# Moving one unit of row maxima between two key blocks of PV on TensorE

## The chip, the cores and the metric

The kernel runs on one core of a Trainium2 chip. The metric is device microseconds of that core, from the median of several runs. The engines are TensorE (PE in the profile; its weight loads are listed apart as PEld), VectorE (DVE), ScalarE (ACT), GpSimd (POOL) and SyncE (SP, which issues most of the DMAs). They run side by side and meet at semaphores. Lines such as L1384 are lines of the kernel before.

## The reference

A transformer layer on 2 sequences of 512 tokens with 128 features: a modulated projection, causal attention with 16 heads of 8 features, an output projection with residual, a mixture of shared and routed experts, and a mixture of zones. The change touches attention alone:

```python
scores = jnp.einsum('bhsd,bhtd->bhst', q, k) / scale
causal = jnp.tril(jnp.ones((S, S), dtype=bool))
scores = jnp.where(causal[None, None], scores, -jnp.inf)
attn = jax.nn.softmax(scores.astype(jnp.float32), axis=-1).astype(x.dtype)
out = jnp.einsum('bhst,bhtd->bhsd', attn, v)
...
x = x + _L0_attn_ref(_L0_cond_ref(x, cond_1024, L0_cond_weight), L0_attn_w_qkv, L0_attn_w_out)
```

## The kernel before

The 2 sequences and 16 heads make 8 groups of four heads (`GROUPS`, `HG`), and the 512 tokens are four blocks of 128 (`KB`). Attention runs in 8 periods, n = 0 to 7. In period n three groups are under way at once:

- Scores for the exponential of group n, with keys along the partitions (`scores_for_exp`, L1422, L1426, L1431). There are six pieces, u = 0 to 5. Each goes through one of two pairs of PSUM banks, so piece u waits until ScalarE's exponential (`exp`, L1089) of piece u - 2 is done. This text calls them E0 to E5.
- Row maxima of groups n+1 and n+2, with queries along the partitions (`scores_for_max`, L1384, L1389). TensorE makes a unit of scores in one of three ring banks (`RING_BANKS`), and VectorE adds the mask and reduces it (`reduce_max`, L753). A unit waits until VectorE has reduced the unit three places earlier in the ring. From group 2 on a group has eleven units, and the last of them, number 10, is the one with the diagonal blocks of token block 0 of all four heads: one matmul of 512 columns (L1384), four reductions of 128 columns. This text calls it the diagonal unit. After it VectorE places the group's maxima (`place_max`, L766, L768), and TensorE lays them under the queries (`lay_max_under_q`, L1399), which ScalarE copies out (`copy_qm`, L1093).
- PV of group n-1 (`weigh_v`, L1447): probabilities times values, key block by key block, all into one bank. The four heads take 32 columns of the array each and run at the same time. A float32 matmul is done in two passes, so a key block shows as 8 matmuls in the trace, in two halves of four. Block 0 is done in period n-1, blocks 1, 2 and 3 in period n. When block 3 is done, ScalarE copies the bank out (`copy_pv`, L1099), between E1's exponential and E2's.

`maximum(i)`, i = 0 to 10, issues a period's share of units (`max_units`). In periods 1 to 6 `maximum(3)` is exactly the diagonal unit of group n+1. In period 0 it is an ordinary unit and there is no PV of an earlier group; in period 7 it is empty. The order on each engine is the order in which the code is written; nothing reorders it. The part of a period that matters here, on TensorE:

```python
scores_for_exp(n, 1)
maximum(1)
maximum(2)
if n:
    weigh_v(n - 1, 1, P, S)
    weigh_v(n - 1, 2, 2 * P, S)
    weigh_v(n - 1, 3, 3 * P, S)
maximum(3)
scores_for_exp(n, 2)
...
scores_for_exp(n, 3)
maximum(4)
maximum(5)
maximum(6)
scores_for_exp(n, 4)
```

`maximum(4)` to `maximum(6)` are units 0, 1 and 2 of group n+2; unit 2 is three places behind the diagonal unit in the ring. After E4 come PV block 0 of group n, unit 3, the laying of the maxima, unit 4, E5, unit 5 (three places behind unit 3, the laying counts as a place) and unit 6.

Of the kernel before, what the change touches and what calls it, by code (L numbers as in the profile page):

```python
# [68 lines left out]
def max_units(n, i):  # L69

    first, end = units_to(n + 1, LEAD if n else FIRST), units_to(n + 2, LEAD)
    return MX_LIST[first + (end - first) * i // SLICES:first + (end - first) * (i + 1) // SLICES]
# [78 lines left out]
def program(nc, io, scratch, out):  # L151
# [9 lines left out]
    with ctx:  # L161
# [1101 lines left out]
        def _(pe):  # L1263
# [103 lines left out]
            def scores_for_max(n, u):  # L1367
                s = n % 2
                pieces = MX_UNITS[n][u]
                if n == 0:  # L1370
                    if u < 2 * HG:
                        pe.wait_ge(q0_placed, u + 1)
                    if u in (0, HG):
                        pe.wait_ge(rep_copied, 1 + u // HG)
                elif u == 0:
                    pe.wait_ge(q_padded[s], 16 * HG * ((n + 1) // 2))
                    pe.wait_ge(ld_stack[n][1], 16)
                wait_ring("max", n, u)
                bank = ring("max", n, u)
                if len(pieces) == HG:  # L1380
                    pe.wait_ge(ld_stack[n][0], 16)
                    for padded in k_padded[n % BUFS]:
                        pe.wait_ge(padded, 32 * (n // BUFS + 1))
                    last = T.matmul(bank.rearrange("p (j k) -> p j k", j=HG), q_mov[n % BUFS][0:TOP, 0:P],  # L1384
                                    k_pad[n % BUFS][0:TOP, :, 0:P], start=True, stop=True)
                else:
                    for j, qb, o in pieces:
                        width = max(2 * P, P * (qb + 1))
                        last = T.matmul(bank[:, o:o + width], q_pad[s][0:TOP, j, qb * P:(qb + 1) * P],  # L1389
                                        stacked[0:TOP, n, 0:width], start=True, stop=True)  # L1390
                last.then_inc(mx_full, 1)

            def lay_max_under_q(n):
                pe.wait_ge(m_ready, n + 1)
                wait_ring("lay", n)
                if n == 0:
                    pe.wait_ge(const_ready, 1)
                for qb in range(KB):
                    last = T.matmul(ring("lay", n)[:, qb * P:(qb + 1) * P], max_pad[n % 2][:, qb, :], ident_b[:],  # L1399
                                    start=True, stop=True)  # L1400
                last.then_inc(qm_full, 1)

            def scores_for_exp(n, u):
                s = n % BUFS
                c, h2 = divmod(u, 2)
                if u == 0:
                    pe.wait_ge(qm_copied, n + 1)
                    if n == 0:
                        pe.wait_ge(rep_copied, 4)
                    else:  # L1410
                        pe.wait_ge(ld_stack[n][0], 16)
                    if n < BUFS:
                        pe.wait_ge(ones_rows[s], 16)
                if c == 0:
                    pe.wait_ge(k_padded[s][h2], 32 * (n // BUFS + 1))
                wait_slot("exp", n, u)
                at_ = slot_of("exp", n, u)
                q = q_mov[s][0:ROWS, :]
                if c < 2:
                    for i in range(2):  # L1420
                        k = k_pad[s][0:ROWS, 2 * h2 + i, c * P:(c + 1) * P]
                        last = T.matmul(ST[:, at_ + i, 0:S - c * P], k, q[:, c * P:S], start=True, stop=True)  # L1422
                elif h2 == 0:
                    for j in range(HG):
                        o = j % 2 * 2 * P
                        last = T.matmul(ST[:, at_ + j // 2, o:o + 2 * P], k_pad[s][0:ROWS, j, 2 * P:3 * P], q[:, 2 * P:S],  # L1426
                                        start=True, stop=True)
                else:
                    pe.wait_ge(q1_zero, 2)
                    pe.wait_ge(q_last_ready, n + 1)  # L1430
                    last = T.matmul(ST[:, at_, :].rearrange("p (j q) -> p j q", j=HG), stacked[0:ROWS, n, 3 * P:S],  # L1431
                                    q_last[0:ROWS], start=True, stop=True)
                last.then_inc(st_full, 1)

            def weigh_v(n, kb, lo, hi):
                c = min(kb, 2)
                pe.wait_ge(masked, 3 * n + c + 1)
                if kb == 0 and lo == 0:
                    pe.wait_ge(v_copied, KB * (n // NG + 1))
                    if n:  # L1440
                        pe.wait_ge(pv_copied, n)
                    else:
                        pe.wait_ge(xc_ready[2], 1)
                o = lo - kb * P + (2 * P if kb == 3 else 0)
                for j in range(HG):
                    v0 = ((n * KB + kb) * HG + j) * VC
                    last = T.matmul(PV[32 * j:32 * j + 32, lo:hi], v_all[:, v0:v0 + 32],  # L1447
                                    probs[n % 2][:, c, j, o:o + hi - lo], start=(kb == 0 and lo == 0),
                                    stop=(kb == KB - 1), skip_group_check=True)
                if kb == KB - 1:  # L1450
                    last.then_inc(pv_full, 1)
# [25 lines left out]
            def project_out(b):  # L1477
                pe.wait_ge(onorm_ready, b + 1)
                pe.wait_ge(ld_small, 16)
                if b == 0:  # L1480
                    wait_ring("out", 0)
                    T.matmul(ring("out", 0), small[:, W_OUT:W_OUT + D], packed_out[:],
                             start=True, stop=True).then_inc(proj_ready, 1)
                else:
                    pe.wait_ge(last_norm, 1)
                    T.matmul(MISC, small[0:EARLY, W_OUT:W_OUT + D], packed_out[0:EARLY, :], start=True, stop=False)
                    T.matmul(MISC, small[:, W_LAST:W_LAST + D], o_sb[1][:], start=False,
                             stop=True).then_inc(proj_ready, 1)
# [15 lines left out]
            def route_experts(b):  # L1504
                pe.wait_ge(temb_ready, B)
                pe.wait_ge(x1_ready, b + 1)
                if b == 0:
                    wait_ring("route", 0)
                bank = ring("route", 0) if b == 0 else MISC
                T.matmul(bank[:, 0:KB * EXPERTS], temb[:, b, :], small[:, W_RT:W_RB], start=True, stop=True)  # L1510
                for t in range(KB):
                    last = T.matmul(bank[:, t * EXPERTS:(t + 1) * EXPERTS],
                                    x1[:, b * S + t * P:b * S + (t + 1) * P], small[:, W_R:W_RT],
                                    start=False, stop=True, skip_group_check=True)
                last.then_inc(logits, 1)
# [99 lines left out]
            for n in range(GROUPS):  # L1615

                def maximum(i):
                    for unit in max_units(n, i):
                        scores_for_max(*unit)

                scores_for_exp(n, 0)
                maximum(0)
# [3 lines that stand above are left out]
                if n:  # L1626
                    weigh_v(n - 1, 1, P, S)
                    weigh_v(n - 1, 2, 2 * P, S)
                    weigh_v(n - 1, 3, 3 * P, S)
                maximum(3)  # L1630
                scores_for_exp(n, 2)
                if n == GROUPS - 1:
                    project_out(0)
# [5 lines that stand above are left out]
                if n == GROUPS - 1:  # L1639
                    route_experts(0)  # L1640
                weigh_v(n, 0, 0, S)
                maximum(7)
                if n + 1 < GROUPS:
                    lay_max_under_q(n + 1)
                if n == 0:
                    project_v(1)
                maximum(8)
                scores_for_exp(n, 5)
                maximum(9)
                maximum(10)  # L1650
# [109 lines left out]
```

## Time and profile before

| what | value |
|---|---|
| median of 3 runs | 188.44 us |
| lowest and highest | 186.72 and 188.64 us |
| the profiled execution | 187.13 us |
| its span, first to last instruction | 185.4 us |
| TensorE busy | 171.9 us (93%) |
| VectorE busy | 148.0 us (80%) |
| ScalarE busy | 134.4 us (72%) |
| GpSimd busy | 93.9 us (51%) |

The span is what the trace covers; the 1.7 us between it and the execution's own time lie around it. Attention takes the span's part from about 25 to 97 us, the experts and zones what follows. A timeline row gives the start, the length, the engine, the line, the shapes and a count where equal instructions are merged; in brackets the idle time of the engine just before and what ended it.

### The profile page before, as it was taken

What the parts mean: (1) busy time and instruction counts of PE and PEld (TensorE: products, weight loads), DVE (VectorE), ACT (ScalarE), POOL (GpSimd) and SP (SyncE); (2) the same over time, 40 slices, a digit from 0 to 9 for tenths busy, and PEclk for the clock granted to TensorE, in tenths of its full rate; (3) what the DMA queues carried; (4) which work ended last, traced back from release to release, by engine and by line L of the source; (5) the groups of instructions that cost most, each with busy time, mean ns of one, the idle gap of its engine ahead of it and who ended that gap; (6) DMA issues with size and microseconds to landing.
All of it is one profiled execution on the core that took longest, in us unless ns stands there. A gap on an engine that the chain in (4) does not pass through costs nothing.

```text
span 185.4 us, 3258 instructions
## 1 busy us (share of the span) xinstructions
PE 171.9 (93%) x934; PEld 118.1 (64%) x934; DVE 148.0 (80%) x458; ACT 134.4 (72%) x224; POOL 93.9 (51%) x102
## 2 busy tenths in 40 slices
PE   7998989899999999989999999896996999999993
PEld 2755565565666667653658767674674867788881
DVE  5589899879898899992697998798999847656652
ACT  4569267667777888889634986945559999799980
POOL 4509086894453858587422522022838980677000
PEclk9999999999999999999999999999699999999998
DMA  4824765757666657520122999930940000001001
GB/s 140 284 44 107 200 175 142 226 182 243 190 216 187 170 185 192 170 81 1 57 53 66 257 333 319 347 91 11 280 167 0 0 4 0 0 2 57 0 4 57
DMA packets 15205, 24.28 MB, mean 131 GB/s; under 512 B 2700, under 2 KB 4684, under 8 KB 15164
## 3 DMA queue, kind: packets, MB, share of 16 engines
q1 hardware_dynamic: 14388, 23.29, 41.4%
q10 hardware_dynamic: 800, 0.79, 1.6%
q8 instruction: 8, 0.13, 0.3%
q14 instruction: 9, 0.07, 0.1%
HBM read 18.71 MB, written 5.27 MB: 129 GB/s over the span
## 4 chain that ended last, share of the span: by engine, by line
PE 59%; issue 10%; DVE 8%; POOL 8%; ACT 6%; SPq 5%; DMA 2%; POOLq 0%; DVEq 0%; ACTq 0%
PE psum L1519 9%; PE psum L1389 8%; PE psum L1520 8%; PE psum L1521 8%; PE psum L1447 8%; PE psum L1422 6%; POOL t_q_pad L686 3%; ACT t_probs L1089 2%; SPq L430 2%; SPq L443 2%; PE psum L1325 2%; PE psum L1271 2%; DMA scratch<-t_dn_lo 2%; PE psum L1384 1%; PE psum L1426 1%
## 5 line engine op out<-in xcount | busy, mean ns | idle before, releaser
L753 DVE CUSTOM_DVE_ANT_0 psum<-psum,t_causal 128x128 f32<-128x128 f32 (+3 forms) x128 | 58.7, 521 | 4.7 <-PE psum L1384 2.6
L1089 ACT ACTIVATE t_probs<-psum 128x1024 f32<-128x1024 f32 (+2 forms) x48 | 40.7, 882 | 8.9 <-PE psum L1422 5.2
L1389 PE MATMUL psum<-t_stacked,t_q_pad 96*128 96x256 f32 (+2 forms) x104 | 31.9, 377 | 2.2 <-DVE t_row_max L753 1.0
L655 POOL TENSOR_SCALAR_AFFINE_SELECT t_probs<-t_probs 128x512 f32<-128x512 f32 x32 | 20.9, 666 | 22.7 <-ACT t_probs L1089 20.7
L1389 PEld LDWEIGHTS psum<-t_stacked,t_q_pad 96*128 96x128 f32 x104 | 17.7, 188 | 16.3 <-DVE t_row_max L753 11.1
L928 DVE SCALAR_TENSOR_TENSOR t_q_pad<-psum,t_zw_all,t_q_pad 128x512 fp32r<-128x512 f32 x24 | 17.9, 749 | 10.2 <-ACT t_q_pad L1137 10.2
L1447 PE MATMUL psum<-t_probs,t_v_all 128*32 128x512 f32 (+3 forms) x256 | 20.8, 439 | 0.4 <-POOL t_probs L655 0.4
L686 POOL TENSOR_TENSOR t_q_pad<-t_raw,t_q_pad 128x512 fp32r<-128x512 f32 x8 | 10.7, 1344 | 20.3 <-ACT t_q_pad L1139 20.3
L753 DVE DVE_READ_ACCUMULATOR2_ANT t_row_max<- 128x1 f32 x128 | 18.0, 140 | 0.0
L1137 ACT ACTIVATE t_q_pad<-psum,t_zw_all 128x512 fp32r<-128x512 f32 x24 | 16.6, 690 | 0.8
L1123 ACT ACTIVATE t_raw<-psum 128x512 f32<-128x512 f32 x24 | 14.3, 598 | 3.7 <-PE psum L1521 3.6
L915 DVE TENSOR_TENSOR psum<-t_raw,t_stacked 128x512 f32<-128x512 f32 x16 | 15.2, 956 | 0.7 <-DVE t_top L836 0.7
L1519 PE MATMUL psum<-t_stacked,t_up_hi 128*128 128x512 f32 x32 | 14.3, 446 | 0.8 <-DVE t_q_pad L931 0.7
L1123 ACT ACTIVATE psum<-psum 128x512 f32<-128x512 f32 x24 | 14.1, 588 | 0.0
L1422 PE MATMUL psum<-t_q_two,t_k_pad 104*128 104x512 f32 (+1 forms) x48 | 13.6, 382 | 0.4 <-ACT t_q_two L1093 0.4
L1520 PE MATMUL psum<-t_stacked,t_up_lo 128*128 128x512 f32 x32 | 12.8, 401 | 0.0
L1521 PE MATMUL psum<-t_stacked,t_up_hi 128*128 128x512 f32 x32 | 12.8, 401 | 0.0
L1447 PEld LDWEIGHTS psum<-t_probs,t_v_all 128*32 128x32 f32 x256 | 6.4, 109 | 8.6 <-POOL t_probs L655 3.4
L1139 ACT CAST t_q_pad<-psum 128x512 fp32r<-128x512 f32 x16 | 9.4, 587 | 3.1 <-DVE psum L915 2.7
L1519 PE MATMUL psum<-t_q_pad,t_dn_hi 128*128 128x512 f32 x24 | 10.0, 416 | 1.7 <-ACT t_probs L1149 1.6
L931 DVE TENSOR_TENSOR t_q_pad<-psum,t_q_pad 128x512 fp32r<-128x512 f32 x16 | 10.9, 678 | 0.8 <-ACT t_q_pad L1139 0.8
L1422 PEld LDWEIGHTS psum<-t_q_two,t_k_pad 104*128 104x128 f32 x48 | 8.5, 189 | 2.4 <-issue 0.9
(230 smaller groups left out, 378.1 us busy)
## 6 DMA issues: line engine op xcount, KB each, us to landing
t_stacked<-scratch SPq DMA_DIRECT2D x16, 256.0 KB, 5.4
t_probs<-in_L_ffn_Wa SPq DMA_DIRECT2D x2, 1024.0 KB, 12.5
scratch<-t_o_sb SPq DMA_DIRECT2D x7, 256.0 KB, 2.1
t_raw<-in_experts SPq DMA_DIRECT2D x7, 256.0 KB, 3.2
t_stacked<-scratch SPq DMA_DIRECT2D x9, 192.0 KB, 2.8
t_q_pad<-scratch SPq DMA_DIRECT2D x28, 48.0 KB
scratch<-t_dn_hi SPq DMA_DIRECT2D x2, 512.0 KB, 3.3
t_q_two<-scratch SPq DMA_DIRECT2D x5, 192.0 KB, 2.5
```

The costliest lines, as they stand in the source:

```text
L655: last = G.affine_select(out=tri, in_=tri, compare_op=ALU.is_ge, fill=0.0, base=0, pattern=[[0, HG], [1, P]], channel_multiplier=-1)
L753: last = V.tensor_tensor_reduce(scores, scores, causal[:, S - width:S], 1.0, 3 * BIG, ALU.add, ALU.max, row_max[s][:, qb, j:j + 1])
L928: V.scalar_tensor_tensor(h_lo[i % SLOTS], hidden_of(i), weight_of(i), f32_of(h_hi[i % SLOTS]), ALU.mult, ALU.subtract).then_inc(lo_done, 1)
L1089: A.activation(o, scores, ACT.Exp, scale=float(1.0 / np.sqrt(np.float32(HD)))).then_inc(exp_done, 1)
L1123: A.activation(o, pair_of(i)[:, 0, :], func, scale=scale).then_inc(act_done, 1)
L1137: A.activation(h_hi[i % SLOTS], hidden_of(i), ACT.Identity, scale=weight_of(i)).then_inc(hi_done, 1)
L1389: last = T.matmul(bank[:, o:o + width], q_pad[s][0:TOP, j, qb * P:(qb + 1) * P], stacked[0:TOP, n, 0:width], start=True, stop=True)
L1422: last = T.matmul(ST[:, at_ + i, 0:S - c * P], k, q[:, c * P:S], start=True, stop=True)
L1447: last = T.matmul(PV[32 * j:32 * j + 32, lo:hi], v_all[:, v0:v0 + 32], probs[n % 2][:, c, j, o:o + hi - lo], start=(kb == 0 and lo == 0), ...
L1519: T.matmul(o, hi, x_hi, start=start, stop=False)
L1520: T.matmul(o, lo, x_hi, start=False, stop=False)
L1521: return T.matmul(o, hi, x_lo, start=False, stop=stop)
```

## The change

The diagonal unit is written between PV blocks 2 and 3 in place of behind block 3:

```diff
                 if n:
                     weigh_v(n - 1, 1, P, S)
                     weigh_v(n - 1, 2, 2 * P, S)
+                maximum(3)
+                if n:
                     weigh_v(n - 1, 3, 3 * P, S)
-                maximum(3)
                 scores_for_exp(n, 2)
```

TensorE in period 4, at the place of the edit (L1447 is PV, block 2 with 256 columns and block 3 with 128; L1384 is the diagonal unit; L1422 is E2; in brackets the semaphores waited for):

```order
 L1447 MATMUL psum<-t_probs,t_v_all 32x256 [waits masked]
 L1447 MATMUL psum<-t_probs,t_v_all 32x256 x3
-L1447 MATMUL psum<-t_probs,t_v_all 32x128 [waits masked]
-L1447 MATMUL psum<-t_probs,t_v_all 32x128 x3
 L1384 MATMUL psum<-t_stacked 128x512 [waits k_padded2a,k_padded2b,ld_stackq5,mx_reduced]
+L1447 MATMUL psum<-t_probs,t_v_all 32x128 [waits masked]
+L1447 MATMUL psum<-t_probs,t_v_all 32x128 x3
 L1422 MATMUL psum<-t_q_two,t_k_pad 128x384 [waits exp_done]
 L1422 MATMUL psum<-t_q_two,t_k_pad 128x384
```

The unit now stands with matmuls of 32 columns on both sides, and block 3 with matmuls of 128 columns on both sides. The same difference stands in periods 1, 2, 3, 5 and 6, six in all, and nowhere else.

What follows on TensorE in period 4, the same before and after the change (L1389 are units 0, 1 and 2 of the next group, L1426 is E4, L1447 is PV block 0):

```order
 L1389 MATMUL psum<-t_stacked,t_q_pad 128x256 [waits mx_reduced]
 L1389 MATMUL psum<-t_stacked,t_q_pad 128x256
 L1389 MATMUL psum<-t_stacked,t_q_pad 128x384 [waits mx_reduced]
 L1426 MATMUL psum<-t_q_two,t_k_pad 128x256 [waits exp_done]
 L1426 MATMUL psum<-t_q_two,t_k_pad 128x256 x3
 L1447 MATMUL psum<-t_probs,t_v_all 32x512 [waits pv_copied,v_copied,masked]
```

Nothing moved here. The 384-column unit waits for VectorE to reduce the diagonal unit, and L1426 waits for ScalarE's exponential of E2.

ScalarE in period 4, the same before and after the change (L1099 is the copy of PV, L1089 are exponentials, L1184 is a copy for the experts):

```order
L1089 ACTIVATE t_probs<-psum 128x1024 [waits st_full]
L1099 COPY t_o_sb<-psum 128x512 [waits stored1,pv_full]
L1089 ACTIVATE t_probs<-psum 128x2x384 [waits st_full]
L1184 CAST t_up_hi<-t_raw 128x512 [waits ld_raw2]
L1089 ACTIVATE t_probs<-psum 128x2x384 [waits st_full]
```

Nothing moved here either: the copy that waits for PV block 3 stands ahead of E2's exponential.

## Rows read from the trace of the kernel before

**Rows 1.** Busy time of each engine in period 4 (windows).
```profile
core 0: us, PE busy (x) PEld busy (x) DVE busy (x) ACT busy (x) POOL busy (x), PEclk, DMA share, GB/s
61.07:69.44 8.37, 8.36 (x64) 5.34 (x63) 7.76 (x35) 7.06 (x11) 5.95 (x7) 1.00 0.56 163
```

**Rows 2.** The chain that ended last, from 60 to 72 us, by line.
```profile
by line: PE psum L1389 38.0%; PE psum L1447 26.6%; PE psum L1422 21.5%; PE psum L1399 4.0%; PE psum L1426 3.9%; PE psum L1431 3.9%; PE psum L1384 3.6%; issue 0.1%
```

**Rows 3.** Timeline of PE in period 4, E1 to unit 5.
```profile
61.92 0.64 PE L1422 MATMUL psum<-t_q_two,t_k_pad 104*128 104x512 f32 x2
62.40 0.63 PE L1389 MATMUL psum<-t_stacked,t_q_pad 96*128 96x512 f32 x2
62.96 1.50 PE L1447 MATMUL psum<-t_probs,t_v_all 128*32 128x384 f32 x24
64.39 0.50 PE L1384 MATMUL psum<-t_stacked 96*128 96x512 f32 x1
64.73 0.87 PE L1422 MATMUL psum<-t_q_two,t_k_pad 104*128 104x384 f32 x4
65.44 1.08 PE L1389 MATMUL psum<-t_stacked,t_q_pad 96*128 96x256 f32 x5
66.36 0.63 PE L1426 MATMUL psum<-t_q_two,t_k_pad 104*128 104x256 f32 x4
66.92 1.06 PE L1447 MATMUL psum<-t_probs,t_v_all 128*32 128x512 f32 x8
67.92 0.44 PE L1389 MATMUL psum<-t_stacked,t_q_pad 96*128 96x384 f32 x1
...
69.08 0.68 PE L1389 MATMUL psum<-t_stacked,t_q_pad 96*128 96x384 f32 x2
```

**Rows 4.** Timeline of the weight loads (PEld), period 4.
```profile
63.30 0.13 PEld L1447 LDWEIGHTS psum<-t_probs,t_v_all 128*32 128x32 f32 x4 [0.19 <-issue]
63.63 0.56 PEld L1447 LDWEIGHTS psum<-t_probs,t_v_all 128*32 128x32 f32 x12 [0.19 <-issue]
64.06 0.13 PEld L1447 LDWEIGHTS psum<-t_probs,t_v_all 128*32 128x32 f32 x4
64.39 0.19 PEld L1384 LDWEIGHTS psum<-t_stacked 96*128 96x128 f32 x1 [0.20 <-issue]
...
66.08 0.19 PEld L1389 LDWEIGHTS psum<-t_stacked,t_q_pad 96*128 96x128 f32 x1 [0.22 <-DVE t_row_max L753]
```

**Rows 5.** Timeline of DVE, period 4: the diagonal unit, then unit 3.
```profile
64.93 0.30 DVE L753 CUSTOM_DVE_ANT_0 psum<-psum,t_causal 128x128 f32<-128x128 f32 x1 [0.53 <-PE psum L1384]
...
65.89 0.14 DVE L753 DVE_READ_ACCUMULATOR2_ANT t_row_max<- 128x1 f32 x1
...
68.39 0.58 DVE L753 CUSTOM_DVE_ANT_0 psum<-psum,t_causal 128x384 f32<-128x384 f32 x1
68.89 0.14 DVE L753 DVE_READ_ACCUMULATOR2_ANT t_row_max<- 128x1 f32 x1
```

**Rows 6.** Timeline of ACT, period 4: copy of PV, exponential of E2.
```profile
64.53 0.59 ACT L1099 COPY t_o_sb<-psum 128x512 f32<-128x512 f32 x1 [0.67 <-PE psum L1447]
65.28 0.81 ACT L1089 ACTIVATE t_probs<-psum 128x768 f32<-128x768 f32 x1 [0.17 <-PE psum L1422]
```

**Rows 7.** Timelines of PE and ACT, period 6: E2, E4, E2's exponential.
```profile
81.48 0.86 PE L1422 MATMUL psum<-t_q_two,t_k_pad 104*128 104x384 f32 x4
82.90 0.74 PE L1426 MATMUL psum<-t_q_two,t_k_pad 104*128 104x256 f32 x4 [0.56 <-ACT t_probs L1089]
...
82.03 0.81 ACT L1089 ACTIVATE t_probs<-psum 128x768 f32<-128x768 f32 x1 [0.17 <-PE psum L1422]
```

**Rows 8.** Timelines of PE and DVE, period 1: unit 3 and its reduction.
```profile
42.59 0.44 PE L1389 MATMUL psum<-t_stacked,t_q_pad 96*128 96x384 f32 x1
...
43.24 0.60 DVE L753 CUSTOM_DVE_ANT_0 psum<-psum,t_causal 128x384 f32<-128x384 f32 x1
```

**Rows 9.** Timeline of SP's queue, period 4: the query loads for group 7.
```profile
69.16 1.61 SPq L430 DMA_DIRECT2D t_q_pad<-scratch  x4
```

## The prediction

> **What bounds the kernel now.** I read the windows first, one period of attention at a time. In period 4 TensorE is busy for 8.36 of 8.37 us and VectorE for 7.76 [rows 1], and the chain that ended last runs from 60 to 72 us over TensorE's lines alone [rows 2]. So the time of a period is the time of TensorE's list, and what counts is what its starts hide: the ends of matmul rows are modelled, the starts are not. I therefore read differences of starts. Two 512-column matmuls take 0.48 us (61.92 to 62.40), 0.24 each; four of 384 take 0.71 (64.73 to 65.44), 0.18 each [rows 3]. Against these, four places cost more than their columns.
>
> Switch in, from 128 to 32 columns: the last two units before PV take 62.40 to 62.96, 0.56 where 0.48 is their price, so 0.08. By the same 0.08 the four 256-column matmuls of E4 (66.36 to 66.92) are 0.12 each [rows 3]. The first tiled half of PV then takes 0.34 (62.96 to 63.30) and the second 0.33 (to 63.63), 0.01 more [rows 3, 4].
>
> Switch out, from 32 to 128: the loads for the second half of block 3 start at 64.06, when its first half starts to stream. Two halves of block 2 took 0.43 (63.63 to 64.06), so two of block 3, with half the columns, take 0.22 and end at 64.28. The diagonal unit's weights load only from 64.39: 0.11 later [rows 4].
>
> Uncovered load: a matmul whose weights were not loaded under the one before costs 0.10 more. The diagonal unit takes 0.34 (64.39 to 64.73) where 0.24 is the price [rows 3].
>
> The wait for VectorE: TensorE is through unit 1 at 65.44 + 4 x 0.12 = 65.92, but unit 2 needs the diagonal unit reduced, and that ends at 65.89 + 0.14 = 66.03. Its load starts at 66.08 and it streams at 66.18, 0.26 after it could have [rows 3 to 5]. VectorE for its part sat idle 0.53 us until the diagonal unit was there [rows 5].
>
> **The change, part by part.** Nothing is added or removed; per period one matmul of 512 columns changes places with eight of 128. VectorE's, ScalarE's, GpSimd's and SP's lists stay as they are.
>
> The diagonal unit comes earlier. Block 2 ends at 64.06, the switch out takes 0.11, so its load starts at 64.17 in place of 64.39. Its reductions move by the same 0.22, within VectorE's idle 0.53, and end at 65.81.
>
> TensorE's list gets longer, by one more pass in each direction. From 64.17: unit 0.34, switch in 0.08, block 3 0.01 + 0.22, switch out 0.11, uncovered load of E2 0.10. E2 streams at 65.03 in place of 64.73: **0.30 us later**. Before, E2's weights were loaded under the diagonal unit; that cover is gone.
>
> The Trainium skill's page "TensorEngine Tiling (Array Packing)", section "Tiling Modes", says that changing the tiling mode, not just the tile, drains TensorE. It speaks against this change, gives no price, and the 0.08 and 0.11 above are what a switch shows in this trace. The page "TensorE: Matmul & The Clock Gate", section "Single matmul latency", puts a drain at about 175 ns; as an estimate from that figure the two added switches would cost 0.35 in place of 0.19, and the change 1 us more over six periods. No row shows so much, and the rows decide.
>
> The wait at unit 2 goes. TensorE is there at 65.92 + 0.30 = 66.22, VectorE done at 65.81, and unit 2's weights load under unit 1. It streams at 66.22 in place of 66.18. Up to here the period loses 0.04 in place of 0.30.
>
> What is late next is E4. It uses the banks of E2 and waits for ScalarE's exponential of it. Before, that ended at 65.28 + 0.81 = 66.09, just in time to load E4 under unit 2 [rows 6]. Now it starts 0.30 later by E2, at 65.58. Ahead of it on ScalarE stands the copy of PV, which waits for block 3, and block 3 ends at 64.82 in place of 64.28, 0.54 later. So the copy starts at 64.53 + 0.54 = 65.07, occupies ScalarE for 0.58 (64.53 to 65.28, less the 0.17 idle before 65.28), and lets the exponential start at 65.65. It ends between 66.39 and 66.46. In period 6, where E4 waits for it already, the load follows 0.06 after the exponential's end (82.03 + 0.81 to 82.90) [rows 7]. So E4 loads at 66.45 to 66.52, uncovered, and streams 0.10 later, at 66.55 to 66.62 in place of 66.36: **0.19 to 0.26 us a period**.
>
> Behind E4 nothing gives it back. PV block 0 and unit 3 follow; unit 3's scores are ready at 67.92 + 0.44 = 68.36, VectorE starts on them at 68.39 and ends at 68.89 + 0.14 = 69.03, and unit 5 starts at 69.08 [rows 3, 5]. This piece hangs on unit 3 alone, so it moves as a whole. Earlier reductions before it only turn into a longer wait at unit 5.
>
> Of DMAs only the store of the PV copy moves, by 0.54. Queued behind it on SP are among others the query loads for group 7, issued by 69.16 + 1.61 = 70.77 [rows 9]. They are used by unit 0 of period 5, one period after 65.44, at 73.8 [rows 1, 3], which itself gets later. I count them as nothing; without that 3 us of cover each 0.1 us would cost 0.1.
>
> The sum. Periods 2 to 5 are alike: 4 x 0.19 to 0.26 is 0.76 to 1.04. In period 6 E4 waits for the exponential anyway (idle 0.56) [rows 7], so nothing is absorbed: 0.30, or 0.37 if the copy comes last. In period 1 VectorE started on unit 3 at 43.24 although it was ready at 42.59 + 0.44 = 43.03; less the 0.03 of reaction it had 0.18 in hand and now comes earlier, so that period pays 0.01 to 0.08 [rows 8]. Periods 0 and 7 are untouched. Together 1.07 to 1.49; I take the middle, 1.3, since copy and E2 come within 0.07 of each other. Everything after attention depends on what precedes it and moves along. The profiled execution would take 187.13 + 1.3 = 188.4, the median 188.44 + 1.3 = **189.7 us**.
>
> **The rivals.** Slower by more: block 3 alone is short. Its halves of 0.11 are shorter than the loading of four weights, 0.13 in the rows of 63.30 and 64.06 [rows 4]. In the middle of PV these loads are hidden under longer halves; behind the diagonal unit up to 0.12 more could stand open, at most one load of 0.13 less the 0.01 counted. That delays block 3, the copy and E2 alike, 0.12 x 6 = 0.7: 190.4 in all. It decides from about 0.1 a period, where the loss passes 1%. Against it: the first half of block 1 showed only 0.01.
>
> Not slower, first: the switch is hidden. If the diagonal unit's weights could load under block 2 and block 3's under the unit, E2 would not move, the wait at unit 2 would go, and E4 would start when the exponential lets it: loading 0.06 after 66.09, streaming at 66.25, 0.11 earlier. Five periods give -0.55: 187.9. The row of 64.39 speaks against it, since that load waited although nothing but the switch held it ("issue", 0.20) [rows 4]. The page on TensorE, section "Step-by-step: what each phase is for", says that weight loads are pulled ahead of matmuls in flight when they go to the background buffer; by that rule this rival would hold, and the trace agrees only among matmuls of one kind.
>
> Not slower, second: VectorE is the real pace. Then its 0.22 comes off each of periods 1 to 5, and period 6 pays 0.30: -0.8, 187.6. For it speaks the wait at unit 2, against it the idle 0.53 on VectorE and that unit 5 hangs on unit 3.
>
> That the change doesn't do what it says is excluded by the order: the swap stands in six periods.
>
> **How the numbers follow.** Forecast 0.67, the short block 3 0.20, hidden switch 0.07, VectorE's pace 0.06. The runs before lie between 186.72 and 188.64, so a median may be off by some 0.7 and this kernel hardly tells less than 1% (1.9 us) from no change. The range takes the forecast and the first rival: from 189.5 less the scatter and some room, 188.3, to 190.4 plus some scatter, 190.8. Slower by over 1% means above 190.3: half of the first rival and some scatter of the forecast, 0.21. Faster by over 1% needs more than either rival gives, 0.03. Within 1%: 0.76.
>
> **What the profile after would show.** In periods 2 to 5 the diagonal unit's row starts some 0.33 after block 2's last half started; a second gap of about 0.1 opens in front of E2; unit 2 has no idle time behind VectorE; E4 (L1426) has some, ended by ScalarE's L1089; a period takes about 8.6 us. I am wrong if E2's load is covered, if E4 shows no wait, or if the period grows by the full 0.30.

## The result, and the profile after

The changed kernel took 190.82 us in the median of 5 runs (190.56 to 192.14), the kernel before 188.61 in 5 (186.72 to 190.83): a ratio of 1.0187 with a 95% interval of 1.0125 to 1.0249. It is slower, by more than was forecast, and its median lies 0.02 us above the range. Its profiled execution took 192.14 us, with a span of 190.4 us. Here and below a ratio goes by the times near the fastest of each kernel, medians and means go by all times, so a ratio is not their quotient (1.0117 for these two medians).

Yet attention did what was forecast. Busy time of each engine in periods 2 to 4 of the changed kernel, each from the start of E5 to the next (windows):

```profile
core 0: us, PE busy (x) PEld busy (x) DVE busy (x) ACT busy (x) POOL busy (x), PEclk, DMA share, GB/s
45.91:54.51 8.60, 8.58 (x64) 5.13 (x63) 7.92 (x35) 6.17 (x9) 3.51 (x5) 1.00 0.52 164
54.51:63.07 8.56, 8.55 (x63) 5.12 (x63) 7.91 (x35) 6.57 (x10) 4.03 (x6) 1.00 0.59 172
63.07:71.64 8.57, 8.55 (x63) 5.13 (x63) 7.92 (x35) 7.01 (x11) 5.95 (x8) 1.00 0.63 189
```

A period is 0.20 us longer (8.57 against 8.37 [rows 1]), and TensorE is busy all through it. Periods 3 to 5 take 8.56 to 8.60 us in every trace of the changed kernel. The timeline of TensorE in period 4, changed kernel:

```profile
65.18 0.62 PE L1389 MATMUL psum<-t_stacked,t_q_pad 96*128 96x512 f32 x2
65.73 1.28 PE L1447 MATMUL psum<-t_probs,t_v_all 128*32 128x384 f32 x16
66.94 0.50 PE L1384 MATMUL psum<-t_stacked 96*128 96x512 f32 x1
67.38 0.43 PE L1447 MATMUL psum<-t_probs,t_v_all 128*32 128x128 f32 x8
67.73 0.96 PE L1422 MATMUL psum<-t_q_two,t_k_pad 104*128 104x384 f32 x4
68.53 0.80 PE L1389 MATMUL psum<-t_stacked,t_q_pad 96*128 96x256 f32 x5
69.25 0.72 PE L1426 MATMUL psum<-t_q_two,t_k_pad 104*128 104x256 f32 x4
```

Its weight loads, and VectorE's and ScalarE's timelines at the same place:

```profile
66.40 0.13 PEld L1447 LDWEIGHTS psum<-t_probs,t_v_all 128*32 128x32 f32 x4 [0.19 <-issue]
66.94 0.19 PEld L1384 LDWEIGHTS psum<-t_stacked 96*128 96x128 f32 x1 [0.41 <-DVE t_row_max L753]
67.37 0.16 PEld L1447 LDWEIGHTS psum<-t_probs,t_v_all 128*32 128x32 f32 x8 [0.25 <-issue]
67.73 0.65 PEld L1422 LDWEIGHTS psum<-t_q_two,t_k_pad 104*128 104x128 f32 x4 [0.20 <-issue]
...
69.25 0.30 PEld L1426 LDWEIGHTS psum<-t_q_two,t_k_pad 104*128 104x128 f32 x2 [0.17 <-ACT t_probs L1089]
...
65.75 0.14 DVE L753 DVE_READ_ACCUMULATOR2_ANT t_row_max<- 128x1 f32 x1
...
67.48 0.30 DVE L753 CUSTOM_DVE_ANT_0 psum<-psum,t_causal 128x128 f32<-128x128 f32 x1 [0.30 <-PE psum L1384]
71.38 0.57 DVE L753 CUSTOM_DVE_ANT_0 psum<-psum,t_causal 128x384 f32<-128x384 f32 x1 [0.26 <-PE psum L1389]
...
67.87 0.59 ACT L1099 COPY t_o_sb<-psum 128x512 f32<-128x512 f32 x1 [1.26 <-PE psum L1447]
68.39 0.81 ACT L1089 ACTIVATE t_probs<-psum 128x768 f32<-128x768 f32 x1
```

The reader is to see four things. The unit (66.94) and block 3 (67.37, 67.38) each start behind a gap of their own, and E2's weights load only at 67.73, when its matmul is due. The bracket of 66.94 names VectorE, but the reduction that the unit has to wait for, three places earlier in the ring, was over at 65.75 + 0.14 = 65.89, so VectorE does not make this gap. Unit 2 no longer stands behind VectorE: the five L1389 from 68.53 run on, where one waited until 66.08 before [rows 3, 4]. E4's weights wait 0.17 for ScalarE's L1089, which they did not before. And VectorE still waits, now also 0.26 us at 71.38 for unit 3, so its earlier start is worth nothing behind E4.

Where the rest of the time went is seen in windows at places that the change doesn't touch. Changed kernel:

```profile
18.70:25.50 6.80, 6.68 (x16) 3.60 (x14) 3.70 (x13) 1.18 (x5) 2.05 (x2) 0.50 0.78 193
145.00:148.40 3.40, 3.40 (x9) 2.65 (x10) 3.23 (x7) 2.30 (x5) 3.32 (x3) 0.51 0.00 0
```

Kernel before, the first of these stretches:

```profile
18.70:25.50 6.80, 5.87 (x28) 3.53 (x27) 6.10 (x29) 2.37 (x6) 2.40 (x2) 1.00 0.84 215
```

The column PEclk is the granted clock. At 0.50, the lower of the two levels, TensorE got through 16 matmuls where it did 28 at full clock. The first stretch lies ahead of the first moved instruction, and it alone puts E4 of period 0 at 32.29 us in place of 29.88.

### The profile page after: what moved, and what is told of

Read it like the earlier page. It is cut to its first block, busy times and chain, and to the rows that moved or that the text cites. A ratio compares the mean times of both kernels' runs of the same rounds, so it can differ in the third digit from the quotient of the medians.

```text
span 190.4 us, 3258 instructions
## 1 busy us (share of the span) xinstructions
PE 175.4 (92%) x934; PEld 118.4 (62%) x934; DVE 148.7 (78%) x458; ACT 133.9 (70%) x224; POOL 93.8 (49%) x102
## 4 chain that ended last, share of the span: by engine, by line
PE 64%; DVE 14%; issue 7%; ACT 7%; POOL 6%; POOLq 0%; DVEq 0%; ACTq 0%
PE psum L1389 9%; PE psum L1519 9%; PE psum L1447 8%; PE psum L1520 8%; PE psum L1521 8%; PE psum L1422 7%; DVE psum L753 5%; POOL t_q_pad L686 4%; PE psum L1339 3%; ACT t_probs L1089 2%; PE psum L1325 2%; PE psum L1271 2%; PE psum L1426 2%; PE psum L1384 1%; PE psum L1349 1%
## 5 line engine op out<-in xcount | busy, mean ns | idle before, releaser
L1089 ACT ACTIVATE t_probs<-psum 128x1024 f32<-128x1024 f32 (+2 forms) x48 | 40.8, 882 | 7.7 <-PE psum L1422 5.1
L1389 PE MATMUL psum<-t_stacked,t_q_pad 96*128 96x256 f32 (+2 forms) x104 | 32.1, 390 | 2.0 <-DVE t_row_max L753 1.2
L1389 PEld LDWEIGHTS psum<-t_stacked,t_q_pad 96*128 96x128 f32 x104 | 18.3, 199 | 16.2 <-DVE t_row_max L753 10.2
L1447 PE MATMUL psum<-t_probs,t_v_all 128*32 128x512 f32 (+3 forms) x256 | 21.8, 441 | 0.0
L915 DVE TENSOR_TENSOR psum<-t_raw,t_stacked 128x512 f32<-128x512 f32 x16 | 14.6, 917 | 1.8 <-ACT t_raw L1123 1.0
L1422 PE MATMUL psum<-t_q_two,t_k_pad 104*128 104x512 f32 (+1 forms) x48 | 14.0, 390 | 0.4 <-ACT t_q_two L1093 0.4
L1447 PEld LDWEIGHTS psum<-t_probs,t_v_all 128*32 128x32 f32 x256 | 5.9, 108 | 8.2 <-issue 4.3
L1422 PEld LDWEIGHTS psum<-t_q_two,t_k_pad 104*128 104x128 f32 x48 | 8.2, 188 | 3.0 <-issue 1.7
```

Source lines behind the costliest of these rows:

```text
L1089: A.activation(o, scores, ACT.Exp, scale=float(1.0 / np.sqrt(np.float32(HD)))).then_inc(exp_done, 1)
```

## The experiments

Each ran against the kernel before on the same chip. The table gives the mean and the ratio with its interval, and from the one trace of each the time from E5 of period 1 to E5 of period 7 (attention, which leaves out period 1), from there to the end (behind), and the start of E4 of period 0 (head). In e_best the new order stands in period 0 too, so its head is not comparable.

| run | times | mean us | ratio (95%) | head | attention | behind |
|---|---|---|---|---|---|---|
| before, first profile | | | | 29.88 | 49.22 | 92.44 |
| changed, first profile | 5 | 191.09 | 1.0187 (1.0125 to 1.0249) | 32.29 | 50.51 | 93.97 |
| c_before | 12 | 189.28 | 1.0073 (1.0017 to 1.0128) | 32.17 | 49.25 | 93.99 |
| c_before_2 | 12 | 188.23 | 1.0003 (0.9956 to 1.0051) | 32.15 | 49.24 | 92.46 |
| c_after | 6 | 190.24 | 1.0140 (1.0047 to 1.0234) | 29.92 | 50.32 | 94.03 |
| c_after_2 | 6 | 189.80 | 1.0100 (1.0038 to 1.0163) | 29.96 | 50.38 | 94.00 |
| c_after_3 | 12 | 189.69 | 1.0109 (1.0066 to 1.0151) | 32.17 | 50.55 | 93.97 |
| e_mid | 12 | 189.77 | 1.0110 (1.0056 to 1.0164) | 32.27 | 50.60 | 93.99 |
| e_switch | 6 | 189.47 | 1.0130 (1.0045 to 1.0215) | 29.88 | 50.84 | 92.47 |
| e_five | 12 | 190.02 | 1.0073 (1.0027 to 1.0120) | 29.96 | 50.09 | 93.99 |
| e_best | 12 | 189.47 | 1.0060 (1.0020 to 1.0099) | 29.16 | 49.77 | 94.04 |
| e_delay | 6 | 190.12 | 1.0103 (1.0018 to 1.0188) | 31.91 | 50.55 | 93.97 |
| e_delay_2 | 6 | 189.64 | 1.0110 (1.0034 to 1.0187) | 29.80 | 50.51 | 92.44 |
| e_early | 12 | 188.02 | 1.0030 (0.9989 to 1.0071) | 30.69 | 48.96 | 93.99 |
| f_before | 12 | 188.31 | 1.0009 (0.9950 to 1.0069) | 29.89 | 49.25 | 93.03 |
| f_after | 12 | 188.43 | 1.0016 (0.9972 to 1.0059) | 31.97 | 50.54 | 92.49 |
| f_early | 12 | 187.09 | 0.9948 (0.9904 to 0.9991) | 30.08 | 49.19 | 92.46 |

**The control and the changed kernel again.** No edit.

> The kernel before, unchanged, as a control for scatter. Theory A (the change costs what its attention periods show, 6 periods at about 0.19, some 1.1 us; the rest of the 2.2 us between the first medians is where stretches of the lower TensorE clock happen to fall): single times spread over some 4 us, as 186.7 to 190.8 did, and the periods 2 to 5 take 8.37 to 8.39 us. Theory B (the change costs another 1 us or more outside attention in every execution): the times of this kernel stay near 188.6.

> The changed kernel, unchanged, once more. Theory A: periods 2 to 5 take 8.57 us again, outside attention its stretches of full clock are as long as before's, and its median lies 1.0 to 1.3 us above the control's, a ratio of about 1.006. Theory B: the median lies 2.2 to 3.5 us above the control's again, a ratio of 1.012 to 1.019, and a stretch outside attention is longer at full clock.

> The kernel before once more, to compare with the changed kernel on the same chip. Theory A (the change costs its attention periods, 1.2 us; where the stretches of the lower TensorE clock fall is chance, the same for both kernels): single times between 186 and 191 us in groups about 1.5 us apart, and behind attention either 92.4 or 94.0 us, by whether a stretch of the lower clock falls on busy matmuls at about 143 to 148 us. Theory B (the change itself costs more behind attention): always 92.4.

> The changed kernel once more. Theory A: from the end of period 1 to the end of period 7 it takes 1.1 to 1.3 us more than the kernel before, and everything else is one of the same few values (ahead of attention 29.9 or 32.2 us, behind it 92.4 or 94.0); over all times of both kernels the difference comes towards 1.2 us, 0.6 to 0.7%. Theory B: behind attention 94.0 us always, and 2 us or more between the kernels.

> The changed kernel once more. If the 0.6 us between its mean excess so far (1.8) and what attention shows in each trace (1.1 to 1.3) is chance, these times are on average 1.2 us above the kernel before, with some below 188; if it belongs to the change, 1.8 us or more, with none below 188.

The kernel before, compared with itself, came out at 1.0073 with an interval that leaves out 1, and the second time at 1.0003; its single times in all jobs lie between 186.09 and 191.14 us. Its trace in c_before has both lower stretches that the changed kernel's first trace had (windows, kernel before, execution of c_before):

```profile
18.00:25.00 7.00, 6.88 (x17) 3.79 (x16) 4.19 (x14) 1.10 (x6) 1.82 (x5) 0.52 0.79 178
...
144.00:148.00 4.00, 4.00 (x12) 3.13 (x11) 3.58 (x7) 2.93 (x6) 3.92 (x4) 0.57 0.00 0
```

So those two are no property of the change. Its other trace, of c_before_2, has the lower clock behind attention elsewhere, and full clock where c_before had the lower one:

```profile
130.90:134.90 4.00, 4.00 (x13) 2.78 (x12) 3.97 (x4) 2.37 (x5) 3.27 (x3) 0.58 0.86 275
144.00:148.00 4.00, 4.00 (x19) 3.23 (x18) 4.00 (x7) 3.76 (x7) 3.98 (x3) 1.00 0.00 0
```

The 14 traces without the fillers that come last below all have just one such stretch between attention and the last microseconds. In four it lies between 129 and 136 us and the part behind attention takes 92.44 to 92.47 us; in ten it lies between 142 and 149 us and that part takes 93.97 to 94.04.

The execution of c_before and the changed kernel's first have the same head (32.17 and 32.29) and the same part behind attention (93.99 and 93.97), and their spans are 189.1 and 190.4 us: 1.3 apart. Attention takes 49.22 to 49.25 us in three traces of the kernel before and 50.32 to 50.55 in four of the changed one, 1.07 to 1.33 more. Theory A has its numbers there. That all four traces of the changed kernel have 94.0 behind attention is what theory B had.

Now the times. Over 133 of the kernel before (mean 188.55) and 29 of the changed one (190.07) the difference is 1.52 us, give or take 0.49 at 95%. Without the first five of each, which raised the question, it is 1.31, give or take 0.52, over 24 times of the changed kernel: near attention's value, and 2 lies outside. Each execution also has a mean granted clock. Among those with at most 0.973 the changed kernel lies 1.06 above the kernel before (8 and 40 times, give or take 0.53), among the others 1.36 (16 and 88 times, give or take 0.39). The expectations for single jobs were met in part. In the first job c_after came out at 1.0140, as theory B had it, though the control beside it was at 1.0073, and their medians (190.18 and 189.11) are 1.07 apart, as theory A had it. The mean of c_after_3 is 1.3 above that job's 23 times of the kernel before (188.36), but none of the 12 lies below 188.

In the two traces of the changed kernel at full clock up to attention, E5 to E5 of period 2 takes only 8.42 and 8.44 us (windows of periods 2 and 3, c_after):

```profile
43.89:52.31 8.42, 8.42 (x63) 5.13 (x63) 7.78 (x35) 6.00 (x9) 3.51 (x5) 1.00 0.58 174
52.31:60.87 8.56, 8.55 (x63) 5.12 (x63) 7.93 (x35) 6.58 (x10) 4.03 (x6) 1.00 0.59 169
```

That is the marker: in period 2 E5 comes 0.17 earlier before unit 5, which waits longer for VectorE behind it.

**The unit between blocks 1 and 2.**

```diff
                 if n:
                     weigh_v(n - 1, 1, P, S)
+                maximum(3)
+                if n:
                     weigh_v(n - 1, 2, 2 * P, S)
                     weigh_v(n - 1, 3, 3 * P, S)
-                maximum(3)
```

> The diagonal unit between PV blocks 1 and 2 in place of 2 and 3. As many switches as in the changed kernel, but both parts of PV are long. If the price is the switches and the uncovered load of E2 (0.30), with E4 then waiting for E2's exponential, a period takes 8.57 us as in the changed kernel, since an earlier diagonal unit helps nothing that ends last. If the short block 3 on its own was part of the price, a period takes up to 0.1 less, about 8.47.

Periods 2 to 5 took 8.60, 8.63, 8.58 and 8.60 us. With both parts of PV long the price is the same, so no part of it is seen to come from the short block 3.

**Another unit between blocks 1 and 2.**

```diff
-                maximum(2)
                 if n:
                     weigh_v(n - 1, 1, P, S)
+                maximum(2)
+                if n:
                     weigh_v(n - 1, 2, 2 * P, S)
```

> The kernel before with another unit, the last of maximum(2) (512 columns), moved from ahead of PV to between blocks 1 and 2; the diagonal unit stays behind block 3. This adds the same pass out of and into 32 columns without the earlier diagonal unit. By the price per switch (0.11 out, 0.10 uncovered load, 0.08 + 0.01 in) TensorE's list grows by 0.30, and the wait for VectorE at unit 2 moves along, so nothing is absorbed: a period of 8.68 us, 6 x 0.30 = 1.8 us in all. If the switches cost little and the changed kernel's 0.19 came from E2's exponential alone, a period stays at 8.38 to 8.45.

Windows of periods 3 and 4 of this kernel, E5 to E5:

```profile
52.47:61.19 8.72, 8.70 (x64) 5.24 (x63) 7.88 (x35) 6.66 (x10) 4.35 (x6) 1.00 0.58 175
61.19:69.90 8.71, 8.69 (x64) 5.22 (x63) 7.88 (x35) 7.04 (x11) 5.93 (x8) 1.00 0.60 172
```

8.71 us, 0.34 more than before where 0.30 was worked out. The pass out of 32 columns and back costs that by itself; the changed kernel, at 8.57, gets 0.14 of it back through the wait at unit 2. From E4 of period 0 to E5 of period 7 it takes 64.73 us, 1.67 more than the kernel before, where 1.8 was expected.

**The swap in periods 1 to 5 alone.**

```diff
                     weigh_v(n - 1, 2, 2 * P, S)
+                if n < GROUPS - 2:
+                    maximum(3)
+                if n:
                     weigh_v(n - 1, 3, 3 * P, S)
-                maximum(3)
+                if n >= GROUPS - 2:
+                    maximum(3)
```

> The swap in periods 1 to 5 alone; period 6 keeps the diagonal unit behind block 3. Periods 2 to 5 as in the changed kernel, 8.57 us. From E5 of period 5 to E5 of period 6 it took 7.55 us before and 8.06 with the change, 0.51 more. If that is period 6's own swap (0.30 to 0.37) and a wait carried over from period 5 (unit 5 behind E5, about 0.17), it takes 7.72 here; if it is all the swap's, 7.55.

From E5 of period 5 to E5 of period 6 it took 7.72 us, to the hundredth what was expected:

```profile
78.13:85.85 7.72, 7.16 (x57) 4.10 (x56) 7.52 (x27) 6.84 (x10) 5.45 (x7) 1.00 0.36 125
```

Of the 0.51 that the changed kernel loses there, 0.34 are period 6's swap and 0.17 come over from period 5.

**One PV group behind E2 and the diagonal unit.**

```diff
                 maximum(2)
+                scores_for_exp(n, 2)
+                maximum(3)
                 if n:
                     weigh_v(n - 1, 1, P, S)
                     weigh_v(n - 1, 2, 2 * P, S)
                     weigh_v(n - 1, 3, 3 * P, S)
-                maximum(3)
-                scores_for_exp(n, 2)
...
+                maximum(4)
                 scores_for_exp(n, 3)
-                maximum(4)
                 maximum(5)
-                maximum(6)
                 scores_for_exp(n, 4)
...
-                weigh_v(n, 0, 0, S)
+                maximum(6)
                 maximum(7)
+                weigh_v(n, 0, 0, S)
...
-                if 0 < n < GROUPS - 1:
-                    copy_pv(n - 1)
                 exp(n, 2)
+                if 0 < n < GROUPS - 1:
+                    copy_pv(n - 1)
```

> One group of PV as before, so no added switch, but the diagonal unit still earlier than in the kernel before: E2 stands ahead of the diagonal unit, both ahead of PV blocks 1 to 3; units 0 to 3 are spread around E3 and E4, PV block 0 comes behind unit 3, and ScalarE copies PV behind E2's exponential. If the switches (0.19) and the uncovered load (0.10) are what the changed kernel paid, and the wait at unit 2 and E4's wait for E2's exponential what the kernel before left open, a period takes about 8.22 us, and the time is some 0.6 to 1.0 us below the kernel before. If the earlier diagonal unit is worth nothing, a period stays at 8.38.

Periods 2 to 4 took 8.21, 8.20 and 8.22 us, as expected: without added switches the new order is worth 0.17 a period. It moves E2 as well as the diagonal unit, so what the earlier unit gives by itself is not shown. The whole was not quicker: 189.47 in the mean is 0.9 above the kernel before, with 94.0 behind attention. Period 5 took 8.69 and period 7 8.82 where they took 8.37 and 8.17 before. The timelines of SP's queue and of TensorE show why in the first case:

```profile
65.86 0.34 SPq L463 DMA_DIRECT2D scratch<-t_o_sb  x1
...
69.89 1.61 SPq L430 DMA_DIRECT2D t_q_pad<-scratch  x4
...
73.84 0.50 PE L1389 MATMUL psum<-t_stacked,t_q_pad 96*128 96x256 f32 x2 [0.42 <-DMA t_q_pad<-scratch]
```

Unit 0 waits for the query loads of group 7, the ones of [rows 9]. They stand behind the store of PV (L463), whose copy is later here. Their last issue ends at 71.50, and the unit starts 2.3 us later. In period 7 E2, now ahead of PV, waits 0.42 us for an exponential (87.48).

**The same in periods 1 to 4 only.** The edit is that of e_best under `if 1 <= n <= 4`, with the order of the kernel before elsewhere.

> As e_best in periods 1 to 4 (E2 and the diagonal unit ahead of one undivided PV, period of 8.21 us there), as the kernel before in the others, where e_best met a late load of queries in period 5 (0.42) and a worse order in period 7 (0.65). Periods 2 to 4 at 8.21 us give 0.5 us, periods 5 to 7 stay as before: from E5 of period 1 to E5 of period 7 about 48.7 us against 49.2, and a time about 0.5 us below the kernel before. If the earlier diagonal unit is taken back by the return to the old order, 49.2.

Periods 2 to 4 took 8.22, 8.18 and 8.22 us again, but period 5 took 8.57 and period 6 7.65 (8.37 and 7.55 before), so half of it was given back: attention 48.96 us in place of 48.7. In the mean 188.02, 0.53 below the 133 times of the kernel before, give or take 0.53.

**A later end of attention without the swap.**

```diff
                 wait_slot("exp", n, u)
                 at_ = slot_of("exp", n, u)
                 q = q_mov[s][0:ROWS, :]
+                if (n, u) == (3, 2):
+                    for _ in range(24):
+                        T.matmul(ST[:, at_, 0:P], ident_b[:], ident_b[:], start=True, stop=True)
```

> The kernel before with 24 matmuls of 128 bf16 columns in front of E2 in period 3 (they write a bank that E2 overwrites, and compute nothing that is used), so that attention ends about 1.2 us later and nothing else changes: no added switch. If a later end of attention costs its own length and no more, the mean over the runs lies 1.2 us above the kernel before. If moving the later work by 1.2 us makes it meet the lower TensorE clock more often, the mean lies about 1.8 us above, as the changed kernel's did (190.3 against 188.5 so far), with next to no time below 188.5, and the part behind attention takes 94.0 us.

> The same kernel as in e_delay again, for more times and a second trace; the same expectations.

Attention grew by 1.3 us, as much as the swap adds, and the part behind it took 93.97 us once and 92.44 once. The 12 times together have a mean of 189.88, 1.3 above the kernel before, with a standard error of 0.36, so that both 1.2 and 1.8 are possible. So a longer attention does not force the slower part behind it; whether it makes it more frequent is not told.

**TensorE kept at work in two waits behind attention.** In the kernel before, in the changed one and in e_early:

```diff
+            def fill(i, times):
+                pe.wait_ge(act_done, i - RING + 1)
+                for _ in range(times):
+                    T.matmul(pair_of(i)[:, 0, 0:P], ident_b[:], ident_b[:], start=True, stop=True)
+
             def zone_logits(b):
+                if b == 0:
+                    fill(AT["zone logits"][0], 18)
                 pe.wait_ge(z_tanh, b + 1)
...
             def zone_spread(b):
+                if b == 0:
+                    fill(AT["zone spread"][0], 24)
                 pe.wait_ge(z_w, b + 1)
```

> The kernel before with matmuls that keep TensorE at work in the two waits of the first zone choice (18 and 24 of 128 bf16 columns, ahead of the zone logits and of the spread of the zone weights, where it sat idle 1.40 and 1.77 us; they write a bank that the next unit overwrites, and nothing of them is used). If the 94.0 us that some executions take behind attention come of the lower clock that follows these waits, they vanish: 92.4 us always, no time of 190 us or more, and a mean of 187.7 us. If the lower clock does not depend on what TensorE did there, the two values stay.

> The changed kernel with the same matmuls in the same waits. If the change costs only its attention periods, it now lies 1.1 to 1.3 us above f_before in the mean (188.9), with the part behind attention at 92.4 us. If the change costs more for another reason, 1.6 us or more above f_before (189.3 or more).

> e_early with the same matmuls in the same waits. It should be the quickest of all: attention 0.3 to 0.5 us shorter than the kernel before, 92.4 us behind attention, a mean of 187.3 us. If the filling brings nothing, 188.0 as e_early.

Before, TensorE sat idle 1.77 us ahead of the spread of the weights (timeline, kernel before in c_before), and the lower clock of 144 to 148 us followed:

```profile
143.30 0.38 PE L1612 MATMUL psum<-t_zw,t_ones_row 1*128 1x3 f32 x2 [1.77 <-DVE t_zw L886]
```

The same wait, of 1.67 to 1.76 us, was followed by full clock in the four traces with the earlier stretch, so it does not decide by itself. In f_after there is little idle time left at that place:

```profile
141.61 1.51 PE L1609 MATMUL psum<-t_ident_b 128*128 128x128 bf16 x24
143.53 0.38 PE L1622 MATMUL psum<-t_zw,t_ones_row 1*128 1x3 f32 x2 [0.41 <-DVE t_zw L886]
```

The part behind attention took 93.03, 92.49 and 92.46 us in the three traces; 94.0 did not come up. f_before's trace has the earlier stretch, at 129 to 133 us, ahead of both fillers, so only the other two show a part behind attention without one, up to the last microseconds. No time of the 36 reaches 190 us, as 26 of the 133 of the kernel before do. The swap is in f_after, and behind attention it has the quick value: the swap alone does not make 94.0, and the ten traces above tie that value to the later stretch of the lower clock.

The means missed the expectations: f_before took 188.31 in place of 187.7, and f_after lies only 0.11 above it, give or take 0.78, where 1.1 to 1.3 was expected, which is outside, though attention still takes 50.54 against 49.25 us in the traces. Six of f_before's 12 times, and two of f_after's, have a mean granted clock of 0.982 or less; f_after's own trace, with the lower stretch in the head, has 0.982. So f_before probably met that stretch more often; whether this is all of the gap is not shown. f_early was the quickest of all and beat the kernel before in its own job at 0.9948 (0.9904 to 0.9991). Its trace doesn't credit the order of attention with that (49.19 against 49.22, the gain of three periods lost again in period 5, 8.73 us). The filled waits alone do not explain it either, since f_before has them too; only one of f_early's 12 times has a mean clock of 0.982 or less. What part is fillers and what part chance is open.

## Why the prediction was wrong, and where it held

The step that failed is the allowance for scatter, that a median may be off by some 0.7, and with it the last step of the sum, that everything after attention moves along. The 133 times of the kernel before have a standard deviation of 1.5 us, and medians of five drawn from them one of 0.9, so the difference of two such medians has 1.3. The part behind attention takes 92.4 or 94.0 us in single executions of the same kernel. The sum itself held:

- Switch out: block 2 ends 0.43 after 66.40 and the unit loads at 66.94, 0.11 as put. Switch in with the unit: 66.94 to 67.38, 0.44 for 0.42. Block 3 with its switch out: 67.38 to 67.73, 0.35 for 0.34. E2 uncovered: its four take 0.80 in place of 0.71, 0.09 for 0.10. From the first PV matmul to E2's streaming it is 2.10 (65.73 to 67.73, and 0.10 for the load) where it was 1.77: 0.33 for 0.30.
- The wait at unit 2 went, and E4 came next, as forecast: it loads at 69.25, 0.05 after the exponential's end (68.39 + 0.81), and streams 3.62 us after the first PV matmul in place of 3.40, 0.22 for 0.19 to 0.26.
- The copy of PV and E2 came within hundredths of each other; the exponential follows the copy without idle time.
- Period 1 was put at 0.01 to 0.08 and took about 0.15 at full clock: unit 5 starts at 44.14 in c_after and at 43.95 before, with heads of 29.92 and 29.88.
- The query loads were counted as nothing, with 3 us of cover. They landed in time, but by e_best's wait some 2.3 us of that is their landing, which leaves, as an estimate, 0.7.
- Period 6 lost 0.32 up to E4, with nothing absorbed. The timelines of TensorE there, kernel before and changed kernel, against [rows 7]:

```profile
79.71 1.50 PE L1447 MATMUL psum<-t_probs,t_v_all 128*32 128x384 f32 x24
...
82.90 1.28 PE L1447 MATMUL psum<-t_probs,t_v_all 128*32 128x384 f32 x16
...
86.41 0.74 PE L1426 MATMUL psum<-t_q_two,t_k_pad 104*128 104x256 f32 x4 [0.55 <-ACT t_probs L1089]
```

E4 stands 3.51 us behind the first PV matmul (82.90 to 86.41), where it stood 3.19 (79.71 to 82.90 [rows 7]). From E4 of period 0 to E5 of period 7 the whole is 64.29 and 64.32 us in c_after and c_after_2, 63.06 in the kernel before, all three at full clock: 1.23 to 1.26 where 1.07 to 1.49 was summed and 1.3 taken.

What came on top, 0.9 us between the first medians, was not attention. The forecast read one trace of the kernel before that happened to have its lower clock where it costs little (head 29.88, behind 92.44), and three times between 186.7 and 188.6. In truth the same kernel takes 186.1 to 191.1 us. Of the first five times of the changed kernel four have a mean granted clock of 0.970 to 0.973, as 8 of its later 24 have and 40 of 128 of the kernel before. In the later 24 the executions of the two kinds lie 1.9 us apart (191.15 and 189.21 in the mean), so this alone comes, as an estimate, to about 0.9. All five are at 190.56 or more, which only 7 of the later 24 are, so that independent chance would seldom bring them together; why they came in one job stays open. That the swap shifts the later work so that it meets the lower clock more often was neither shown nor excluded. All four of the changed kernel's own traces have 94.0 behind attention, and one of three of the kernel before.

Of the rivals, the short block 3 fell with e_mid, the hidden switch with e_switch. VectorE's pace fell: in the changed kernel the unit came earlier and the period grew. That the waits left something to gain was right: e_best's order, without the switches, shortens a period by 0.17.

The Trainium skill's page "TensorEngine Tiling (Array Packing)", section "Tiling Modes", has a change of tiling mode drain TensorE: e_switch agrees, where nothing else was added. The gaps here are 0.08 to 0.11 us, and 0.10 more is the weight load that is no longer covered. The estimate from the 175 ns of the Trainium skill's page "TensorE: Matmul & The Clock Gate", section "Single matmul latency", does not fit these gaps.

## What to carry to other kernels

Keep matmuls of one tile shape together: each unit put into a tiled group costs a gap at both of its ends and an uncovered weight load, 0.33 us here, against the wait that it is meant to end. Before a wait is removed, look up what is late next: here the exponential that E4 waits for ended 0.06 us behind VectorE's reduction (66.09 and 66.03), and only about half of the 0.26 us of that wait came back. And run the kernel before against itself before a percent is believed: here it differed from itself by 0.7% once and by nothing once.

## What the hardware showed that was not expected

The same instructions at the same place ran at half the clock in one execution and at full clock in another: 18.7 to 25.5 us at 0.50 in the changed kernel, at 1.00 in the kernel before, at 0.52 from 18 to 25 in the kernel before again. In all three TensorE had worked with the same short gaps just before, 0.16 to 0.22 us each ahead of three matmuls between 15.8 and 17.5 us. A lower stretch there costs 2.1 to 2.4 us at E4 of period 0, of which 1.1 to 2.2 are left at E5 of period 1. One from about 143 to 148 us costs 1.5 us, and one from about 130 to 134 us comes with the quick 92.4 in four traces and with 93.03 in f_before. With short fillers in two waits that precede the later stretch it did not come in three traces; one of these had the earlier stretch, which in four traces without fillers also left the later one out.
